# Second passes of a delta-rule scan: part of one add moved to GpSimd, the query product one token later, u turned one token earlier

## The reference

```python
def step(Sc, inp):
    a11, a12, bt, k, v = inp
    S0, S1 = (Sc[..., 0], Sc[..., 1])
    r0 = a11[..., None] * S0 + a12[..., None] * S1
    r1 = -a12[..., None] * S0 + a11[..., None] * S1
    Sr = jnp.stack([r0, r1], -1)
    err = v - jnp.sum(k * Sr, -1)
    Sn = Sr + bt[..., None, None] * err[..., None] * k
    return (Sn, Sn)
_, Y = jax.lax.scan(step, S0, xs)        # xs: A11, A12, beta, Kh, Vg by position
y = jnp.sum(Q * Y, -1).reshape(b, s, DI)  # Q = (u @ Q_W.T) * sel_C
```

## Time and profile before

| what | value |
|---|---|
| median of three runs | 1680.47 us |
| the profiled execution | 1677.81 us |
| its span from first to last instruction | 1675.6 us |
| VectorE busy | 1267.0 us (76%) |
| TensorE busy | 1248.9 us (75%) |
| ScalarE busy | 409.7 us (24%) |
| GpSimd busy | 68.0 us (4%) |
| mean granted TensorE clock | 0.879 of full speed |
| second pass, batch 0, first product to end of last query product | 430.2 to 616.5 us |
| second pass, batch 1 | 1154.3 to 1340.5 us |

### The profile page before, as it was taken

How to read it: one execution, slowest core, us unless ns; L and a number is a source line. 1 busy time by engine, 2 the same in 40 slices (tenths; PEclk the granted TensorE clock), 3 DMA queues, 4 the chain that set the end, 5 groups by cost and what they waited for, 6 DMA issues and landing times. The chain is left out here.

```text
span 1675.6 us, 12210 instructions
## 1 busy us (share of the span) xinstructions
PE 1248.9 (75%) x4124; PEld 736.0 (44%) x4124; DVE 1267.0 (76%) x1885; ACT 409.7 (24%) x628; POOL 68.0 (4%) x32
## 2 busy tenths in 40 slices
PE   3970554513688888589699999396888786899997
PEld 1440222202344445345465555263544454566665
DVE  4769999998999985758789999987999957100111
ACT  2431000000002015343532232132010143323332
POOL 0000012110000000000001211100000000000000
PEclk9995767656799999779899999698999997999999
DMA  4000100003011120210023222214111010222221
GB/s 151 1 7 0 50 38 38 38 0 126 13 50 38 38 100 6 104 54 7 26 76 101 88 88 76 75 39 176 50 38 39 11 51 1 82 76 78 73 76 75
DMA packets 51676, 94.34 MB, mean 56 GB/s; under 512 B 4640, under 2 KB 39840, under 8 KB 50720
## 3 DMA queue, kind: packets, MB, share of 16 engines
q1 hardware_dynamic: 51616, 93.58, 16.0%
HBM read 73.64 MB, written 19.92 MB: 56 GB/s over the span
## 5 line engine op out<-in xcount | busy, mean ns | idle before, releaser
L486 PE MATMUL ps<-wshare,uT 128*128 128x512 f32 x512 | 244.3, 633 | 55.7 <-DVE kz L1261 55.7
L593 PE MATMUL ps<-kz 128*128 128x256 f32 x1024 | 245.2, 383 | 20.0 <-ACT kz L786 15.4
L579 PE MATMUL ps<-kz 128*128 128x512 f32 x512 | 243.3, 598 | 3.5 <-DMA kz<-in_w 3.3
L593 PEld LDWEIGHTS ps<-kz 128*128 128x128 f32 x1024 | 196.0, 192 | 103.6 <-issue 64.0
L486 PEld LDWEIGHTS ps<-wshare,uT 128*128 128x128 f32 x512 | 101.4, 204 | 178.8 <-issue 117.7
L428 PE MATMUL ps<-wshare,xnT 128*128 128x512 f32 x256 | 146.2, 724 | 35.2 <-ACT ps L661 35.2
L786 ACT ACTIVATE kz<-ps,small 128x512 f32<-128x512 f32 x128 | 87.4, 685 | 296.0 <-PE ps L579 295.8
L1419 DVE TENSOR_TENSOR kz<-ps,b_s 128x256 f32<-128x256 f32 x16 | 6.3, 413 | 180.7 <-PE ps L593 180.7
L579 PEld LDWEIGHTS ps<-kz 128*128 128x128 f32 x512 | 98.3, 193 | 80.6 <-issue 74.6
L420 PE MATMUL ps<-ident,uT 128*128 128x128 f32 x256 | 44.0, 302 | 113.4 <-DVE work L1139 79.1
L721 ACT ACTIVATE kz<-ps 128x512 f32<-128x512 f32 x32 | 19.1, 597 | 371.4 <-PE ps L471 371.4
(11 more groups left out here) (250 smaller groups left out, 1793.4 us busy)
## 6 DMA issues: line engine op xcount, KB each, us to landing
kz<-in_w SPq DMA_DIRECT2D x128, 256.0 KB, 2.9
kap_d<-kz SPq DMA_DIRECT2D x26, 512.0 KB, 2.7
kz<-kap_d SPq DMA_DIRECT2D x26, 512.0 KB, 3.2
uT<-in_x SPq DMA_DIRECT2D x8, 512.0 KB, 5.9
wshare<-in_wq SPq DMA_DIRECT2D x2, 2048.0 KB, 7.8
kz<-in_x SPq DMA_DIRECT2D x2, 2048.0 KB, 12.9
coef<-in_x SPq DMA_DIRECT2D x2, 2048.0 KB, 7.7
wshare<-in_wk SPq DMA_DIRECT2D x2, 1024.0 KB, 11.1
```

Source lines behind the costliest of these rows:

```text
L486: t = mm(ps[:, 2 * (j % 2) + c, :], uT3[:, k, j * P:(j + 1) * P], wq_s[:, k, c, :], start=(k == 0), stop=(k == KI - 1))
L579: t = mm(ps[:, 4 + i % 2, :], w1_r[r][:, k, (f % 2) * P:(f % 2 + 1) * P], x2T[:, k, n * 512:(n + 1) * 512], start=(k == 0), stop=(k == KM ...
L593: t = mm(ps[:, 6 + q // 2, (q % 2) * DM:(q % 2 + 1) * DM], hbuf(i)[:, q * P:(q + 1) * P], w2_r[r][:, f % 2, :], start=(f == 0 and q % 2 == ...
```

## The change

- `turned` is split. GpSimd adds the first 384 of each half's 512 columns (768 elements per partition) and writes them into `k2(j)`; VectorE adds the last 128 (256 elements) between `e = vh - e` and `Y = k * e`. Token 15's sum is still VectorE's alone, now written into `k2`.
- New semaphores: `turn_ready` goes up with `e = Y0 + Y1`, which follows the second `turn`, and starts GpSimd; `turned_ready` goes up with GpSimd's add, and `query` and the next `turn(j, 0)` wait for it.
- `query` multiplies in place in `k2(j)` and comes two tokens behind instead of one: `query(j - 2)` stands in token j. At the end `query(14)` and `query(15)` follow each other, around token 15's sum.
- `value(j + 1)` moves from the token's end to right behind `e = Y0 + Y1`, with two buffers for `vh` in turn.
- `group_stats` comes after tokens 7, 11 and 15 instead of 6, 10 and 14.
- On TensorE u is turned two tokens ahead, and `turn_y(j - 2)` stands before the query projection of token j instead of behind it.

```diff
--- before.py
+++ after.py
+PW = 384
...
@@ -476,10 +479,12 @@
                 pe.wait_ge(wq_loaded, b * 16 + 16)
                 pe.wait_ge(mt_ready, b * 2 + 2)
                 token_u(b, L, 0)
+                token_u(b, L + 1, 1)
                 for j in range(L):
-                    if j + 1 < L:
-                        token_u(b, L + j + 1, j + 1)
+                    if 1 <= j < L - 2:
+                        token_u(b, L + j + 2, j + 2)
                     if j >= 2:
+                        turn_y(b, j - 2)
                         pe.wait_ge(kq_used, 2 * L * b + L + j - 1)
                     for c in range(2):
                         for k in range(KI):
@@ -488,8 +493,7 @@
                     t.then_inc(kq_ready, 1)
                     if j == 0:
                         turn_starts(b)
-                    if j >= 2:
-                        turn_y(b, j - 2)
+                        token_u(b, L + 2, 2)
                 for c in range(2):
                     turn_y(b, L - 2 + c)
                     gate_tile(b, 2 * c)
@@ -839,6 +843,10 @@
                     if i >= 2:
                         pool.wait_ge(sum_ready, b * (L - 2) + i - 1)
                     nc.gpsimd.tensor_tensor(PSt[:, :, 2], PSt[:, :, 2], Z, ALU.add).then_inc(sum_ready, 1)
+                X = tmp[:, 2048:4096].rearrange("p (a i n) -> p a i n", a=2, i=2)
+                for j in range(L - 1):
+                    pool.wait_ge(turn_ready, b * (L - 1) + j + 1)
+                    nc.gpsimd.tensor_tensor(k2(j)[:, :, 0:PW], X[:, :, 0, 0:PW], X[:, :, 1, 0:PW], ALU.add).then_inc(turned_ready, 1)
 
 
         @block.vector
@@ -1237,34 +1245,35 @@
                 st = work[:, 0:1024].rearrange("p (i n) -> p i n", i=2)
                 sr = work[:, 1024:2048].rearrange("p (i n) -> p i n", i=2)
                 Y = tmp[:, 0:1024].rearrange("p (i n) -> p i n", i=2)
-                e, vh = tmp[:, 1024:1536], tmp[:, 1536:2048]
+                e = tmp[:, 1024:1536]
+                vh = [tmp[:, 1536:2048], tmp[:, 4096:4608]]
                 X = tmp[:, 2048:4096].rearrange("p (a i n) -> p a i n", a=2, i=2)
                 at = {}
 
                 def value(j):
                     dve.wait_ge(ut_ready, 2 * L * b + L + j + 1)
-                    if j >= 1:
-                        after(at["e"])
-                    tt(by_head(vh, 0), by_head(ps[:, 4 + j % 2, :], 0), wide(cf[:, CV, j]), MUL).then_inc(ut_used, 1)
+                    if j >= 2:
+                        after(at["s"][j % 2])
+                    tt(by_head(vh[j % 2], 0), by_head(ps[:, 4 + j % 2, :], 0), wide(cf[:, CV, j]), MUL).then_inc(ut_used, 1)
 
                 def turn(j, i):
                     after(at["st"])
-                    at["o"] = mark(tt(by_head(X[:, i], 1), by_head(st, 1), wide(cf[:, H_ + 2 * i:H_ + 2 * i + 2, j]), MUL))
-
-                def turned(j):
-                    after(at["o"])
-                    at["o"] = mark(tt(X[:, :, 0], X[:, :, 0], X[:, :, 1], ADD))
+                    if i == 0 and j >= 1:
+                        dve.wait_ge(turned_ready, b * L + j)
+                    at["t"] = mark(tt(by_head(X[:, i], 1), by_head(st, 1), wide(cf[:, H_ + 2 * i:H_ + 2 * i + 2, j]), MUL))
 
                 def query(j):
-                    after(at["o"])
+                    dve.wait_ge(turned_ready, b * L + j + 1)
+                    if j < L - 1:
+                        after(at["o"])
                     dve.wait_ge(kq_ready, 2 * L * b + L + j + 1)
-                    tt(k2(j), X[:, :, 0], ps[:, 2 * (j % 2):2 * (j % 2) + 2, :], MUL).then_inc(kq_used, 1)
+                    tt(k2(j), k2(j), ps[:, 2 * (j % 2):2 * (j % 2) + 2, :], MUL).then_inc(kq_used, 1)
 
                 dve.wait_ge(start_ready, b + 1)
                 v.tensor_copy(st, ps[:, 6:8, :]).then_inc(start_used, 1)
                 value(0)
                 dve.wait_ge(start_used, b + 1)
-                at["st"] = n_chain[0]
+                at["st"], at["s"] = n_chain[0], {}
                 for j in range(L):
                     k = k2(j)
                     after(at["st"])
@@ -1278,26 +1287,35 @@
                     at["y"] = mark(tt(Y, k, sr, MUL))
                     if j >= 1:
                         turn(j - 1, 1)
-                    after(at["y"])
-                    at["e"] = mark(tt(e, Y[:, 0], Y[:, 1], ADD))
+                        after(at["y"])
+                        tt(e, Y[:, 0], Y[:, 1], ADD).then_inc(turn_ready, 1)
+                    else:
+                        after(at["y"])
+                        at["e"] = mark(tt(e, Y[:, 0], Y[:, 1], ADD))
+                    if j + 1 < L:
+                        value(j + 1)
+                    if j >= 2:
+                        query(j - 2)
                     if j >= 1:
-                        turned(j - 1)
-                    after(at["e"])
+                        dve.wait_ge(turn_ready, b * (L - 1) + j)
+                    else:
+                        after(at["e"])
                     dve.wait_ge(ut_used, 2 * L * b + L + j + 1)
-                    at["e"] = mark(tt(e, vh, e, SUB))
+                    at["e"] = at["s"][j % 2] = mark(tt(e, vh[j % 2], e, SUB))
                     if j >= 1:
-                        query(j - 1)
+                        after(at["t"])
+                        at["o"] = mark(tt(k2(j - 1)[:, :, PW:], X[:, :, 0, PW:], X[:, :, 1, PW:], ADD))
                     after(at["e"])
                     at["y"] = mark(tt(Y, k, e.unsqueeze(1).to_broadcast([P, 2, DI]), MUL))
                     after(at["y"])
                     at["st"] = mark(tt(st, sr, Y, ADD))
-                    if j + 1 < L:
-                        value(j + 1)
-                    if j % 4 == 2 and j > 4:
+                    if j % 4 == 3 and j > 4:
                         group_stats(b, j // 4 - 1)
                 turn(L - 1, 0)
                 turn(L - 1, 1)
-                turned(L - 1)
+                query(L - 2)
+                after(at["t"])
+                tt(k2(L - 1), X[:, :, 0], X[:, :, 1], ADD).then_inc(turned_ready, 1)
                 query(L - 1)
                 dve.wait_ge(kq_used, 2 * L * b + 2 * L)
                 group_stats(b, NCH - 1)
```

More of the change, by code:

```diff
@@ L170, in build @@
         sum_ready = sem("sum_ready")
+        turn_ready = sem("turn_ready")
+        turned_ready = sem("turned_ready")
         out_stored = sem("out_stored")
```

## The result

| | before | after |
|---|---|---|
| median of four runs each | 1679.35 us | 1669.10 us |
| ratio after / before, 95% interval | | 0.9936 [0.9918, 0.9953] |
| profiled execution / its span | 1677.81 / 1675.6 us | 1669.70 / 1666.9 us |
| VectorE busy | 1267.0 us | 1251.8 us |
| GpSimd busy | 68.0 us | 122.5 us |

What follows compares the result with a forecast made beforehand. VectorE was taken to bound the second passes, busy 185.65 of 186.90 us. Per batch -12.1 + 1.1 + 4.6 + 2.4 = -4.0 us, -8.0 for both, from 1677.81 plus 2.7 gave 1672.5 us, range 1661 to 1679.

Steps and rivals of the forecast that it cites:

- What leaves VectorE: In tokens 1 to 15, a 256-element add replaces `turned` on VectorE: 12.1 us less per batch.
- Dependences: In the second passes, VectorE instructions waiting for the result right before them cost net 1.1 us more per batch.
- GpSimd beside VectorE: GpSimd's add holds VectorE's subtraction 0.19 us per usual token, 1.32 in token 1, 0.79 in token 15: 4.6 us per batch.
- the one collision: First pass's last token, kernel before: VectorE's L1176 took 4.31 us instead of 2.28 beside GpSimd; read as mutual exclusion.
- The end: At a pass's end VectorE sits idle 5.6 us instead of 3.23 before the last statistics: 2.4 us more per batch.
- the third rival: TensorE at half clock at the passes' ends: each batch loses 2.5 us more, 1677.5 us; chance 0.10.
- TensorE and the keys: At the new pace of 10.56 us per token, TensorE's work and the key reloads cost nothing.
- The first rival: The subtraction isn't held by GpSimd in the second passes: 1663.3 us; chance 0.18.
- the second: GpSimd's 768-element add gets no shorter, or VectorE is shut out longer: 1687.8 us at 2.34 us per add; chance 0.10.

Runs made afterwards that it cites:

- Experiment 1: Kernel after with GpSimd's loop taken out of the second passes and the whole sum of the turned halves on VectorE: 1686.76 us.
- experiments 2 and 3: Kernel after with GpSimd adding 256 columns per half (1671.38 us), or all 512 with VectorE's part sum left out in tokens 1 to 15 (1678.41 us).
- experiment 6: Kernel after with `turn_y(j - 2)` behind the query projection of token j again on TensorE: 1667.64 us.
- experiment 5: Kernel after with the subtraction moved ahead of `value` and `query`, right behind the add that releases GpSimd: 1666.88 us.
- experiment 10: Kernel after with `query` multiplying by the state tile in SBUF instead of the projection in PSUM, read-out left wrong: 1703.51 us.
- experiment 4: Kernel after with `query` one token behind again, at the token's end, leaving only `value` between GpSimd's start and the subtraction: 1693.81 us.

## Why the prediction was right

The forecast of 1672.5 us lay 3.4 above the measured 1669.1, and -8.0 us for the two passes stands against -10.0 in the traces. The other 1.4 us aren't of the change's making as far as the traces show. I had added 2.7 us for the distance between the profiled execution and the median; for the kernel after this distance is -0.6. Outside the two passes the profiled executions differ by 1.9 us the other way (8.1 apart in all, 10.0 in the passes); two profiled executions of the kernel after, 1669.70 and 1667.19, with passes of the same length, are 2.5 us apart. So the difference of the profiled executions, 8.1, meets the forecast's 8.0 by chance; the passes are the measure.

- *What leaves VectorE, -12.1 us per batch.* Right. Experiment 1 puts it back at 8.6 us net of the held time of 3.4, so 12.0.
- *Dependences, +1.1.* Right, as far as it can be read, as what the others leave: in experiment 1, without GpSimd, the 3.6 us over the kernel before less the end's 2.3 are 1.3.
- *GpSimd beside VectorE, +4.6.* The mechanism was right, the size was off by a quarter. The subtraction's 14.4 us in batch 0 (16 at 898 ns) against 16 x 0.685 are 3.4 us: 0.11 per usual token, 1.23 in token 1, 0.70 in token 15, where 0.19, 1.32 and 0.79 were forecast, 0.08 to 0.09 too much each time. GpSimd starts 0.76 us after the releasing add and not 0.81 (0.07 us after its end; the 0.13 came from an add of the first pass with three semaphores to wait for; that they are the reason was not tried), its record is 1.81 and not 1.83, and VectorE goes on 0.13 and not 0.12 us ahead of its end. Of 0.19 us per token such hundredths are nearly half. In both batches it is 2 x 1.2 = 2.4 us, more than the 2.0 by which the sum was off. That the length of GpSimd's record came out so close has some luck in it: from the one collision I took 2.06 us for 1024 elements and 0.28 fixed, where the sizes of experiments 2 and 3 give 2.16 and 0.2, and at 768 elements the two differences nearly cancel.
- *The end, +2.4.* Right: 5.67 us idle against 5.6 forecast and, in the two batches before, 3.47 and 3.23, so 2.3 more; at the full clock (granted 1.00), as forecast, so the third rival was out.
- *TensorE and the keys, 0.* Right: no idle time of VectorE within the passes, and experiment 6.

The first rival (the subtraction isn't held) falls with experiments 1 to 3, the second (GpSimd's add doesn't scale, or VectorE is shut out for longer) with the records of 1.27, 1.81 and 2.35 us and with VectorE going on 0.13 us ahead of their end. The row of the kernel before that seemed to speak for the first, L1172 unhindered beside GpSimd, is the case of experiment 5: it had begun first. The rule of the Trainium skill, "SBUF — State Buffer", section "SBUF: two separate sides", that whichever side starts first holds the port pair for its whole instruction and the other stands still, agrees with experiments 5 and 10 in kind. Two measurements go another way than its wording: VectorE goes on 0.13 us before GpSimd's record ends, and in token 15 of experiment 10 the waiting side did not get the next turn, though three more VectorE instructions started after it had asked.

## What to carry to other kernels

Work given to GpSimd while VectorE is the bound paid here only under a cover, since GpSimd takes 2.1 ns per element of this add where VectorE takes 1.04. The cover is VectorE instructions with an operand in PSUM, as long together as GpSimd's add. Place them right behind the instruction that releases GpSimd, or behind one short instruction that has begun before GpSimd (experiment 5). Size GpSimd's share to that cover, token by token. Look for the price in durations, not in idle time: a held instruction is recorded as a longer one. When a step is put off by one round, work out what the last round leaves bare, and reorder the end.

## What the runs showed of the hardware

- GpSimd's add of float32 takes 0.2 us and 2.1 ns per element of a partition (0.59 us for 192, 1.27 for 512, 1.81 for 768, 2.35 for 1024), VectorE's 1.04 ns (0.68 us for 512, 1.22 for 1024).
- GpSimd's add and a VectorE instruction that reads two operands from SBUF exclude each other, whichever begins first (subtraction 1.92 us for 0.68 behind GpSimd, GpSimd's add 2.31 for 1.81 behind the subtraction). With one operand in PSUM both run at their full pace (1.21 and 1.81 us).
- A GpSimd add that began 0.16 us after such a VectorE instruction stood 3.0 us (4.80 for 1.80) while four of them followed each other; in experiment 4 one that began 0.05 us after got in behind the first, with 2.31 us.
